# A hardware loop for TensorE's attention batches, and a score-mask wait for each four heads

## What is computed

```python
def _linear_attention(x, W_qkv, b_qkv, W_out, b_out, num_heads=16):
    ...
    q = jax.nn.elu(q * E ** (-0.5)) + EPS_FEAT
    k = jax.nn.elu(k) + EPS_FEAT
    ...
    def step(carry, qkv_t):
        kv_s, k_s = carry
        q_t, k_t, v_t = qkv_t
        kv_s = kv_s + jnp.einsum('bhe,bhf->bhef', k_t, v_t)
        k_s = k_s + k_t
        num = jnp.einsum('bhe,bhef->bhf', q_t, kv_s)
        den = jnp.einsum('bhe,bhe->bh', q_t, k_s)[..., None] + EPS_DEN
        return ((kv_s, k_s), num / den)
...
x = x + 0.5 * ffn(_layernorm(x))      # 64 experts, top 6, and a shared expert
x = x + attention(_layernorm(x))
x = x + 0.5 * ffn(_layernorm(x))
```

## Time and profile before

| | us |
|---|---|
| median of 3 runs | 619.74 |
| the profiled execution | 623.67 |
| its span, first to last instruction | 621.9 |
| attention on TensorE, steps 0 to 7 | about 247 to 392 |
| TensorE busy in the span | 441.1 |
| mean granted clock of TensorE | 0.698 |

### The profile page before, as it was taken

One profiled execution on the slowest core, in us unless ns is written; L12 is line 12 of the kernel. 1 busy time (PEld: TensorE's weight loads), 2 busy tenths in 40 slices (PEclk: granted clock), 3 DMA queues, 4 the chain that ended last, 5 costly groups with the idle time before them and its releaser, 6 DMA issues.

```text
span 621.9 us, 15104 instructions
## 1 busy us (share of the span) xinstructions
PE 441.1 (71%) x5988; PEld 291.9 (47%) x5988; DVE 316.3 (51%) x928; ACT 237.2 (38%) x629; POOL 331.3 (53%) x259
## 2 busy tenths in 40 slices
PE   1894957994798335798978988329757399947960
PEld 1842534552444322676767766229335255424440
DVE  6496952221107973454445564293999322212097
ACT  4961213331233387453534451168611133312420
POOL 6284776888887303022221222003886767888691
PEclk9986865555579556778779795656979655555995
DMA  8988401001029940001110110351000000000492
GB/s 270 380 254 339 180 3 12 5 7 9 4 78 405 408 194 1 3 3 37 37 38 22 38 38 20 92 230 69 1 1 8 6 9 6 9 7 7 157 410 110
DMA packets 34410, 60.74 MB, mean 98 GB/s; under 512 B 12611, under 2 KB 18846, under 8 KB 33870
## 3 DMA queue, kind: packets, MB, share of 16 engines
q1 hardware_dynamic: 23078, 58.41, 26.1%
q0 software_dynamic: 11264, 1.38, 2.4%
HBM read 37.43 MB, written 29.36 MB: 107 GB/s over the span
## 4 chain that ended last, share of the span: by engine, by line
PE 41%; DVE 27%; issue 12%; DMA 12%; ACT 4%; POOL 3%; SPq 1%; POOLq 0%; DVEq 0%; ACTq 0%
DVE X L977 8%; PE bank L780 6%; DMA rows_d<-A 5%; PE upper L797 5%; PE upper L880 5%; DVE Cb L1079 3%; ACT A L510 3%; PE upper L913 2%; PE bank L863 2%; DVE bn L982 2%; DMA Bb<-planes_d 2%; PE upper L926 2%; PE bank L899 2%; PE bank L835 2%; DMA A<-rows_d,tok_i 2%
## 5 line engine op out<-in xcount | busy, mean ns | idle before, releaser
L440 POOL DMA_INDIRECT planes_d<-Bb,put_i x64 | 100.4, 1569 | 26.4 <-issue 19.7
L454 POOL DMA_INDIRECT A<-rows_d,tok_i x64 | 71.9, 1124 | 20.6 <-issue 17.3
L1109 DVE TENSOR_TENSOR ring<-ring,bank 128x88 f32<-128x88 f32 x64 | 15.8, 246 | 107.1 <-ACT ring L578 71.1
L677 PE MATMUL bank<-ident,A 128*128 128x128 f32 x96 | 22.5, 413 | 53.9 <-ACT A L510 39.7
L481 POOL TENSOR_TENSOR Bb<-Cb,chm 128x576 f32<-128x576 f32 x16 | 19.0, 1220 | 76.3 <-PE upper L926 42.5
L481 POOL TENSOR_TENSOR Bb<-w3s,chm 128x576 f32<-128x576 f32 x16 | 17.8, 1147 | 56.2 <-PE upper L926 56.2
L398 POOL TENSOR_TENSOR Bb<-Eb,st 128x512 f32<-128x512 f32 x8 | 8.9, 1113 | 70.3 <-DVE st L1027 70.3
L677 PEld LDWEIGHTS bank<-ident,A 128*128 128x128 f32 x96 | 18.1, 220 | 57.1 <-issue 29.7
L797 PE MATMUL upper<-w2s,ring 88*64 88x128 f32 x256 | 44.0, 448 | 0.1
L1113 DVE TENSOR_SCALAR Bb<-upper,sl 128x128 f32<-128x128 f32 x64 | 22.5, 351 | 30.6 <-PE upper L797 24.5
L880 PE MATMUL upper<-A,Bb 32*32 32x128 f32 x1024 | 35.3, 296 | 2.1 <-issue 2.1
(11 more groups left out here) (179 smaller groups left out, 1098.0 us busy)
## 6 DMA issues: line engine op xcount, KB each, us to landing
planes_d<-zeros SPq DMA_DIRECT2D x8, 2048.0 KB, 20.6
w3s<-in_w3T SPq DMA_DIRECT2D x2, 2816.0 KB
rows_d<-A SPq DMA_DIRECT2D x8, 512.0 KB, 12.1
A<-planes_d SPq DMA_DIRECT2D x8, 512.0 KB, 9.3
PL<-planes_d SPq DMA_DIRECT2D x8, 512.0 KB, 10.0
Cb<-planes_d SPq DMA_DIRECT2D x8, 512.0 KB, 10.8
Bb<-planes_d SPq DMA_DIRECT2D x8, 512.0 KB, 11.9
w1s<-in_w1T SPq DMA_DIRECT2D x1, 2816.0 KB
```

The lines of the kernel that those rows point to most:

```text
L440: pool.indirect_dma_start(out=planes_d[f], in_=Y[:, s, :], in_offset=None, out_offset=bass.IndirectOffsetOnAxis(ap=put_i[:, s:s + 1], axis=0),
L454: pool.indirect_dma_start(out=A[:, t, :], out_offset=None, in_=rows_d, in_offset=bass.IndirectOffsetOnAxis(ap=tok_i[:, t:t + 1], axis=0), ...
L677: ins = pe.transpose(bank[g % 2][:, (i % 4) * P:(i % 4 + 1) * P], A[:, i, :], ident[:, :])
```

## The change

Two edits in TensorE's program. First, `step(b)` waits for the score mask of group g (`sc_sb` at 4b + g + 1) ahead of the first head of that group, instead of for all four ahead of the first head; the waits for `kv_sb` and `sb_ready` stand ahead of the last head's four products instead of behind them. Second, steps 1 to 6 run in a `Fori` of three rounds with two steps each; step 0 and step 7 stay written out. Inside the loop the counts of the waits are computed from the loop's register.

```diff
                 pe.wait_ge(vx_ready, PRIMED + NC * (b + 1))
-                pe.wait_ge(sc_sb, 4 * b + 4)
                 for h in range(HEADS):
+                    if h % 4 == 0:
+                        pe.wait_ge(sc_sb, 4 * b + h // 4 + 1)
+                    if h == HEADS - 1:
+                        pe.wait_ge(kv_sb, PRIMED + NQ * (b + 1))
+                        pe.wait_ge(sb_ready, (NQ - 1) * (b + 1))
                     ob = bank[4 + h // 4][:, 0:NC * GW].rearrange("p (c h f) -> p c h f", c=NC, h=4)
                     for q in range(NQ):
                         o = (h // 4) * L + q * P + (h % 4) * CHUNK
                         pe.matmul(ob[32 * q:32 * q + 32, :, h % 4, :], PR[:, o:o + CHUNK],
                                   VX[:, q, h, :, :], start=(h % 4 == 0), stop=False, skip_group_check=True)
-                pe.wait_ge(kv_sb, PRIMED + NQ * (b + 1))
-                pe.wait_ge(sb_ready, (NQ - 1) * (b + 1))
                 for g in range(4):
...
             step(0, 0, first=True)
-            for b in range(1, B):
-                step(b, b % 2, last=b == B - 1)
+            with pe.Fori(0, (B - 2) // 2) as i:
+                step(2 * i + 1, 1)
+                step(2 * i + 2, 0)
+            step(B - 1, 1, last=True)
             turn_out(B - 1)
             project_out(B - 1)
```

## The result

The changed kernel took 642.74 us (median of 4 runs, 639.79 to 643.87) against 620.01 us beside it: ratio 1.0349, 95% interval 1.0301 to 1.0397. It is slower by about 21.6 us by this ratio (interval 18.7 to 24.6) where 12.8 were forecast. The direction and the mechanism that was named (page fetches of TensorE's code) hold; the size is off by two thirds, and 642.7 lies above the range's end of 641. Three further comparisons, on other chips, gave less, 18.9 to 19.3 us: 1.0309 for the same kernel, 1.0301 with the loop's head held at its old place, and 1.0306 with the old mask wait in the loop. All ratios leave out executions more than 1.5% above the fastest of their kernel, among them three of one_round_c and one of rotated_placed that took 1673 us.

The account below looks back on a forecast made before the run. The prediction took TensorE's attention steps, stalled by code page fetches, to bound the kernel. Its terms, 6.2 + 1.2 + 3.4 + 2.4 - 0.4 = +12.8 us, on the 619.74 us median gave 632.5 us, range 623.5 to 641.

Parts of the forecast that it names:

- What bounds the kernel: TensorE's attention steps: nearly all TensorE, stopped by fetches of its code pages, while the score-mask wait is nearly free.
- 3.6 us per page: TensorE's instruction fetch: a code page is ready 3.6 us after the page ahead of it was entered.
- A, the back edges: Loop branches after steps 2 and 4: each fetches the loop's head again, partly covered by L848; +6.2 us, bounds 0.6 and 10.
- late back edge: Rival at the loop's branches: the next page's fetch must finish first and the clock falls further; +19.8 us, 639.5 us, chance 0.14.
- B, register operations: TensorE's sequencer in the loop: computed wait thresholds take 3.5 us, a third of it exposed; +1.2 us, bounds 0 and 3.5.
- C, the boundaries: Page stalls in steps 1 to 7: rounds repeat the first one's boundaries, step 7 gains a stall; +3.4 us, bounds 0 and 5.
- D, the clock: Project of step 5: stalls ahead of it take away TensorE's full clock; +2.4 us, bounds -1 and +5.
- E, the split wait: Score-mask wait: splitting removes step 0's 0.4 us and nothing elsewhere, the moved waits cost nothing; -0.4 us.
- cheap edge: Rival at the loop's branches: target asked for in time or branch as cheap as DVE's; +4.8 us, 624.5 us, chance 0.14.
- loop at hand: Rival: TensorE holds the loop's pages, so rounds two and three have no page stalls; -5.1 us, 614.6 us, chance 0.07.

Follow-up runs that it names:

- one_round_c: The changed kernel with its two-step body written out three times, each in a loop that runs once; +0.8% (+5.1 us) against the kernel before.
- rotated_placed: The changed kernel with the loop cut behind project, two rounds, and its head at instruction 185 of its page; +1.1% (+7.1 us) against the kernel before.
- hinted_c: The changed kernel with a prefetch hint for the loop's branch; +3.3% (+20.3 us) against the kernel before.
- slot200: The changed kernel with the loop's head at instruction 200 of its page; +1.1% (+6.6 us) against the kernel before.
- paused_c: The kernel before, with TensorE waiting for GpSimd's expanded v at the head of steps 3 and 5, no loop; +1.8% (+10.9 us) against the kernel before.
- placed: The changed kernel with the loop's head at instruction 150 of its page; 0.0% (-0.2 us) against the kernel before.
- rotated: The changed kernel with the loop cut behind project instead of ahead of it, two rounds, a surplus project; +0.2% (+1.2 us) against the kernel before.
- split_only_c: The kernel before with only the split mask wait and moved waits, steps written out; +0.3% (+1.5 us) against the kernel before.
- placed_rounds: The changed kernel with three bodies written out, each head at instruction 150, reached by a jump forward; -0.1% (-0.7 us) against the kernel before.
- mid_rounds: The changed kernel with three bodies at instruction 150, no branch back, and project_out moved between L917's and L928's products; +0.2% (+1.2 us) against the kernel before.

## Why the prediction was wrong

**What bounds the kernel** was right: code pages. 3.6 us per page was right as a size too: where one packet alone comes at the branch, it holds the queue for 3.1 to 4.3 us (hinted_c, slot200, the two rotated kernels with a placed head).

**A, the back edges**, was too small. Forecast 6.2, measured 8.3 (8.2, 8.3 and 9.6 in the three other runs with the loop's head at the same place). The gaps stand where they were forecast, and only L848 covered them. The term had the target asked for at once; the trace has two packets, which I read as the next page's fetch ahead of the target's, and the branches hold the queue for 4.5 to 5.2 us in these runs instead of 3.7. That is the reason of the "late back edge" rival; it adds about 1 us a branch, not 2.2. The Trainium skill (Runtime: NRT & Kernel Launch, Instruction fetch mechanics) describes this stall, and the trace agrees, with these times. The 108 ns that the Trainium skill (Advanced Engine Details and Errata, Control Flow Timing) gives for a compare-and-branch are near the 79 ns of the one that is not taken.

**B, register operations.** Forecast 3.5 us on the queue, 1.2 exposed. The trace has 54 operations of 32 to 53 ns, about 2.0 us on the queue. What of it is exposed can't be told from page waits.

**C, the boundaries**, was right in the sum. B and C together were forecast at 1.2 + 3.4 = 4.6, and page waits grew by 5.2. The six steps of the loop have 16.2 us of them where 14.9 were forecast, step 7 has 1.35 for 2.0, and step 0, which the change hardly touches, has 1.1 more than before. What C missed is what its bounds of 0 to 5 took for granted, that the place of the boundaries matters by a few us of waiting and nothing else: with the head at 150, 200 and 36 the page waits are 14.4, 20.9 and 20.2 us, and between 150 and 36 lie 19 us of time.

**D, the clock, is the step that failed.** Forecast +2.4, bounds -1 to +5; measured +6.2 of busy time, the largest miss of the sum. Step 5's project ran at the lower level as forecast; after the change:

```profile
351.83:357.28 5.45, 5.45 (x13) 3.37 (x14) 0.00 (x0) 2.53 (x4) 0.00 (x0) 0.50 0.02 3
```

But steps 4 and 6, which start behind no branch, lost too: their clock was 0.86 and 0.98 before and is 0.76 in both after. The term tied the clock to the stall ahead of step 5. The runs show that the gaps alone do not bring this loss: the pause of the same length gave +1.4 of busy time (paused_c), and placed keeps gaps of 8.0 us with 123.0 us of busy time, less than before. The other runs with the head at the old place have 129.0, 131.0 and 132.7. So the clock goes with where the boundaries fall, and C and D are not two terms. How the place sets the clock was not settled: rotated had 21.4 us of page waits and the highest clock of all, 0.82. The base was weak as well: in split_only_c, whose time equals before, the project of step 5 took 4.3 us and not the 2.7 of the earlier trace rows, and the stage's busy time was 127.9. Against that the loop's is only 1.1 to 4.8 us more.

**E, the split wait.** Forecast -0.4, measured nothing that can be told (+0.3%, -0.1 to +0.6). No wait on a score mask or on a sum of states appeared in the changed kernel.

**The sum.** In the stage 8.3 (A) + 5.2 (B and C) + 6.2 (D) - 0.7 = 19.0, where 13.2 had stood without E. D is short by 3.8, A by 2.1, B and C by 0.6. The 21.6 us of the first comparison hold some 2 us more, which the three on other chips do not show. The prediction took 0.2% for what can be told from no change; the intervals here are 0.3 to 0.5% to each side. Of the rivals, the cheap edge and the loop at hand are refuted by the branch's 4.5 us and by the packets of queue 8: 32 in steps 1 to 7 (266 to 411 us) against 29 before, 51 in all against 48. The late back edge comes nearest, with +19.8 us and two packets close together, though it has more in A (10.6) and less in D (5) than was measured.

What stays open: how the boundaries' place sets the clock; how the hint shortens the gap; and what the gaps cost by themselves, since 8 us of them cost 11 us in paused_c and placed shows no loss with them. placed_rounds has 3.1 us less of gaps and 1.0 more of page waits than placed, and the intervals of the two ratios (0.3% each, 1.9 us) are too wide to tell whether it gains by that.

## What to carry to other kernels

Where an engine runs short instructions, as TensorE does here with 11 to 17 ns each, its code is a stream with a rate of its own: count the instructions per page against the time that they run, and try slow instructions inside the fast stretch, in one piece. A loop of many pages, like this one of 8.4, pays a fetch at each taken branch, unless enough work is queued when the sequencer gets there (4.1 us of project was enough in rotated, 2.7 in rotated_placed was not). It also repeats one set of page boundaries in all rounds. Before such a loop is judged, try its head at two or three places, for a verdict at one place is a verdict on the place. And count the matmuls of each variant against the base: rotated had 12 too many.

## What was not expected of the hardware

- A taken branch out of the pages at hand holds TensorE's queue for 4.1 to 5.2 us where two packets come with it (eleven branches in six runs), and for 3.1 to 4.3 us where one starts after it (six branches in four runs). The jump forward into a placed body holds it for 0.3 us ahead of step 1, and over some 166 unused slots for 2.1 to 2.7 us ahead of steps 3 and 5 (placed_rounds, mid_rounds).
- The place of a loop's head in its page, 36, 150 or 200, made +3.0%, 0.0% and +1.1% of a 620 us kernel.
- A pause of 8.1 us in two pieces cost 10.9 us (interval 7.8 to 14.0).
- Cutting eight matmuls into four pairs between others cost a third more time for both kinds together (5.5 us for 4.1, both at a granted clock of 0.50).
